# A kernel of sixteen sublayers: the set with logarithm and exponential loaded by an instruction, and the single layer norm in its wide form

## The reference

```python
def _layernorm(x, axis=-1, eps=1e-05):
    m = jnp.mean(x, axis=axis, keepdims=True)
    v = jnp.var(x, axis=axis, keepdims=True)
    return (x - m) / jnp.sqrt(v + eps)
```

```python
def _l2norm(x):                      # l0a, queries and keys
    return x * lax.rsqrt(jnp.sum(x * x, -1, keepdims=True) + 1e-06)
dt = jax.nn.softplus(jnp.einsum('blr,dr->bld', dt_r, W_dt) + b_dt)   # l0b
A = -jnp.exp(A_log)                                                  # l0b
o = (o - mean) * jax.lax.rsqrt(var + EPS)                            # l2a, per head
```

## Time and profile before

| | us |
|---|---|
| median of 3 runs | 3734.16 |
| lowest, highest | 3733.45, 3734.59 |
| profiled execution, its own time | 3737.65 |
| its span in the profile | 3735.9 |

### The profile page before, as it was taken

How to read it: one execution, slowest core, us unless ns; L and a number is a source line. 1 busy time by engine, 2 the same in 40 slices (tenths; PEclk the granted TensorE clock), 3 DMA queues, 4 the chain that set the end, 5 groups by cost and what they waited for, 6 DMA issues and landing times. The chain is left out here.

```text
span 3735.9 us, 56812 instructions
## 1 busy us (share of the span) xinstructions
PE 2940.7 (79%) x22174; PEld 1593.3 (43%) x22242; DVE 1930.9 (52%) x3686; ACT 1391.7 (37%) x2669; POOL 768.4 (21%) x629
## 2 busy tenths in 40 slices
PE   6566777778877599989768888998868568877986
PEld 4454247523356334444422223442333343664555
DVE  5311243478963488710588877113943543636643
ACT  3211533442233256632367776222032112224652
POOL 1000006245526200000554310004600000240003
PEclk9665869878889789999889999997989779878997
DMA  2022001122101422000121100002400001014202
GB/s 105 14 67 64 0 14 43 35 69 68 45 25 43 113 38 41 15 1 0 36 45 30 30 1 1 0 11 57 135 0 0 0 0 45 13 45 87 42 15 68
DMA packets 86478, 136.39 MB, mean 37 GB/s; under 512 B 13319, under 2 KB 52199, under 8 KB 84947
## 3 DMA queue, kind: packets, MB, share of 16 engines
q1 hardware_dynamic: 79187, 118.50, 12.6%
q0 software_dynamic: 7040, 14.43, 1.4%
HBM read 106.81 MB, written 25.85 MB: 36 GB/s over the span
## 5 line engine op out<-in xcount | busy, mean ns | idle before, releaser
L1674 DVE TENSOR_REDUCE at_mp<-PS 128x1 f32<-128x384 f32 (+3 forms) x640 | 313.4, 538 | 115.1 <-PE PS L1524 98.9
L1624 ACT ACTIVATE at_pt<-PS 128x384 f32<-128x384 f32 (+3 forms) x704 | 288.3, 456 | 211.9 <-PE PS L1536 176.7
L1521 PE MATMUL PS<-at_kx,at_qx 72*128 72x384 bf16 (+5 forms) x640 | 218.8, 347 | 67.1 <-DMA at_kx<-L_attn_a_parts 27.2
L1534 PE MATMUL PS<-at_qx,at_kx 105*128 105x512 bf16 (+5 forms) x704 | 214.3, 314 | 7.8 <-ACT at_pt L1624 5.9
L4159 DVE CUSTOM_DVE_ANT_0 PS<-PS,ls_pt 128x1024 f32<-128x1024 f32 x128 | 154.0, 1239 | 19.9 <-ACT ls_pt L4012 16.1
L4012 ACT ACTIVATE ls_pt<-PS,ls_far 128x512 f32<-128x512 f32 x256 | 155.6, 685 | 22.8 <-PE PS L3833 13.5
L2287 DVE TENSOR_TENSOR_SCAN mb_ring<-PS,mb_ring 128x1024 f32<-128x1024 f32 x64 | 146.6, 2291 | 19.3 <-POOL mb_ring L2226 6.6
L2242 PE MATMUL PS<-mb_ring,ident 128*128 128x512 f32 x256 | 148.1, 732 | 5.9 <-DVE mb_ring L2292 5.9
L1005 ACT ACTIVATE mx_h<-PS,small_L 128x128 f32<-128x128 f32 x312 | 87.9, 371 | 150.5 <-PE PS L889 63.8
L889 PE MATMUL PS<-mx_g,mx_w 128*128 128x128 f32 x624 | 98.4, 308 | 53.1 <-DVE mx_w L1082 30.6
L1547 PE MATMUL PS<-at_pt,at_v 128*9 128x256 f32 (+3 forms) x1408 | 130.8, 451 | 5.4 <-issue 1.3
(11 more groups left out here) (822 smaller groups left out, 6752.0 us busy)
## 6 DMA issues: line engine op xcount, KB each, us to landing
rw_arena<-rw_v_rows SPq DMA_DIRECT2D x32, 512.0 KB, 4.6
dl_arena<-in_fir_bank SPq DMA_DIRECT2D x32, 256.0 KB, 3.2
lnA<-mb_rows SPq DMA_DIRECT2D x16, 512.0 KB, 3.6
XN<-mb_rows SPq DMA_DIRECT2D x16, 512.0 KB, 3.7
ffn_place<-in_ffn_L SPq DMA_DIRECT2D x4, 1152.0 KB, 17.0
at_qx<-L_attn_a_parts SPq DMA_DIRECT2D x24, 192.0 KB
at_kx<-L_attn_a_parts SPq DMA_DIRECT2D x72, 64.0 KB
at_qx<-L_attn_b_parts SPq DMA_DIRECT2D x24, 192.0 KB
```

Source lines behind the costliest of these rows:

```text
L1521: mm = nc.tensor.matmul(PS[:, n % 3, 0:e - c], QX[0:RAW, u % 3, g, blk(i, P)], KX[0:RAW, u % 3, g, c:e], start=True, stop=True)
L1534: mm = nc.tensor.matmul(PS[:, 3 + n % 3, 0:e - c], KX[0:FULL, u % 3, g, blk(j, P)], QX[0:FULL, u % 3, g, c:e], start=True, stop=True)
L1624: nc.scalar.activation(PT[:, y % SLOTS, g, 0:e - c], PS[:, 3 + n % 3, 0:e - c], ACT.Exp, scale=SCALE).then_inc(exp_done, 1)
L1674: nc.vector.tensor_reduce(best, sc, AX.X, ALU.max).then_inc(s_maxed, 1)
```

## The change

The layer norm takes the form of the group norm: `center_mat` (the identity less 1/128) centres each block by one matmul, ACT squares out of PSUM, one matmul with `mean_mat` gives the variance on all partitions, ACT makes the logarithm and the exponential of 128x512, and DVE multiplies once.

```diff
@@ -95,6 +95,13 @@
         return scope.enter_context(self.nc.sbuf_tensor(f"{name}_{self.buffers}", shape, dt))
 
 
+LOG_AND_EXP = 6
+
+
+def load_log_and_exp(nc):
+    nc.scalar.add_instruction(mybir.InstLoadActFuncSet(act_func_set_id=LOG_AND_EXP, name=nc.get_next_instruction_name()))
+
+
 def turned_spread(nc, out, cols, ident):
 
     return nc.tensor.matmul(out, cols, ident, start=True, stop=True)
@@ -103,9 +110,8 @@
 def layernorm(k, src, dst, gain=None, shift=None, beside=None):
 
     nc, PS = k.nc, k.PS
-    sq, rstd = k.lnA, k.rstd
-    TB = BLK // P
-    with stage(nc, "mean_ready", "centered", "squared", "var_ready", "std_ready", "rstd_ready", "spread_ready", "scaled", "pool_own") as (block, mean_ready, centered, squared, var_ready, std_ready, rstd_ready, spread_ready, scaled, pool_own):
+    sq, rstd = k.lnA, k.lnA
+    with stage(nc, "centered", "squared", "var_ready", "log_done", "root_done", "scaled", "pool_own") as (block, centered, squared, var_ready, log_done, root_done, scaled, pool_own):
         if beside is not None:
             @block.gpsimd
             def _(pool):
@@ -113,42 +119,41 @@
 
         @block.tensor
         def _(pe):
+            def center(b):
+                nc.tensor.matmul(PS[:, b, :], k.center_mat[:, :], src[:, blk(b)], start=True, stop=True).then_inc(centered, 1)
+
             def variance(b):
                 pe.wait_ge(squared, b + 1)
-                for t in range(TB):
-                    mm = nc.tensor.matmul(PS[:, 4 + b, t:t + 1], sq[:, blk(TB * b + t, P)], k.mean_mat[:, 0:1], start=True, stop=True)
-                mm.then_inc(var_ready, 1)
-
-            def spread(b):
-                pe.wait_ge(rstd_ready, b + 1)
-                for t in range(TB):
-                    mm = turned_spread(nc, PS[:, b, blk(t, P)], rstd[:, TB * b + t:TB * b + t + 1].to_broadcast([P, P]), k.ident[:, :])
-                mm.then_inc(spread_ready, 1)
-
-            for b in range(NBLK):
-                nc.tensor.matmul(PS[:, b, :], k.mean_mat[:, :], src[:, blk(b)], start=True, stop=True).then_inc(mean_ready, 1)
+                nc.tensor.matmul(PS[:, 4 + b, :], k.mean_mat[:, :], sq[:, blk(b)], start=True, stop=True).then_inc(var_ready, 1)
+
+            center(0)
+            center(1)
             variance(0)
-            for b in range(1, NBLK):
-                variance(b)
-                spread(b - 1)
-            spread(NBLK - 1)
+            center(2)
+            variance(1)
+            center(3)
+            variance(2)
+            variance(3)
 
         @block.scalar
         def _(act):
             def square(b):
                 act.wait_ge(centered, b + 1)
-                nc.scalar.activation(sq[:, blk(b)], dst[:, blk(b)], ACT.Square).then_inc(squared, 1)
-
-            def deviation(b):
+                nc.scalar.activation(sq[:, blk(b)], PS[:, b, :], ACT.Square).then_inc(squared, 1)
+
+            def root(b):
                 act.wait_ge(var_ready, b + 1)
-                nc.scalar.activation(rstd[:, TB * b:TB * b + TB], PS[:, 4 + b, 0:TB], ACT.Sqrt, bias=k.eps_col[:, 0:1]).then_inc(std_ready, 1)
-
-            nc.scalar.activation(k.warm[:, 0:1], k.eps_col[:, 0:1], ACT.Sqrt)
+                nc.scalar.activation(rstd[:, blk(b)], PS[:, 4 + b, :], ACT.Ln, bias=k.eps_col[:, 0:1]).then_inc(log_done, 1)
+                act.wait_ge(log_done, b + 1)
+                nc.scalar.activation(rstd[:, blk(b)], rstd[:, blk(b)], ACT.Exp, scale=-0.5).then_inc(root_done, 1)
+
+            load_log_and_exp(nc)
             square(0)
-            for b in range(1, NBLK):
-                square(b)
-                deviation(b - 1)
-            deviation(NBLK - 1)
+            square(1)
+            for b in range(NBLK):
+                root(b)
+                if b + 2 < NBLK:
+                    square(b + 2)
             if gain is not None:
                 for b in range(NBLK):
                     act.wait_ge(scaled, b + 1)
@@ -156,30 +161,9 @@
 
         @block.vector
         def _(dve):
-            def center(b):
-                dve.wait_ge(mean_ready, b + 1)
-                nc.vector.tensor_tensor(dst[:, blk(b)], src[:, blk(b)], PS[:, b, :], ALU.subtract).then_inc(centered, 1)
-
-            def reciprocal(b):
-                dve.wait_ge(std_ready, b + 1)
-                nc.vector.reciprocal(rstd[:, TB * b:TB * b + TB], rstd[:, TB * b:TB * b + TB]).then_inc(rstd_ready, 1)
-
-            def scale(b):
-                dve.wait_ge(spread_ready, b + 1)
-                nc.vector.tensor_tensor(dst[:, blk(b)], dst[:, blk(b)], PS[:, b, :], ALU.mult).then_inc(scaled, 1)
-
-            center(0)
-            center(1)
-            center(2)
-            reciprocal(0)
-            center(3)
-            reciprocal(1)
-            scale(0)
-            reciprocal(2)
-            scale(1)
-            reciprocal(3)
-            scale(2)
-            scale(3)
+            for b in range(NBLK):
+                dve.wait_ge(root_done, b + 1)
+                nc.vector.tensor_tensor(dst[:, blk(b)], PS[:, b, :], rstd[:, blk(b)], ALU.mult).then_inc(scaled, 1)
 
 
 
@@ -2152,7 +2136,7 @@
                     take(b)
                     curve(b - 1)
                 curve(NBLK - 1)
-                nc.scalar.activation(k.warm[:, 0:1], k.eps_col[:, 0:1], ACT.Ln)
+                load_log_and_exp(nc)
                 nc.scalar.activation(A[:, :, :], W[pre + "A_log"], ACT.Exp).then_inc(own_a, 1)
                 keep(0)
                 for b in range(NBLK):
@@ -4282,9 +4269,8 @@
     def sb(n, shape, dt=F32):
         return k.sbuf(st, n, shape, dt)
     k.ident = sb("ident", [P, P])
-    k.mean_mat = sb("mean_mat", [P, P])
+    k.mean_mat, k.center_mat = sb("mean_mat", [P, P]), sb("center_mat", [P, P])
     k.eps_col = sb("eps_col", [P, 1])
-    k.rstd = sb("rstd", [P, NTILE])
     k.rstd2 = sb("rstd2", [P, 2, NTILE])
     k.tiny_col = sb("tiny_col", [P, 1])
     k.warm = sb("warm", [P, 1])
@@ -4312,6 +4298,8 @@
             own(pool.memset(k.ident[:, :], 0.0))
             own(pool.affine_select(out=k.ident[:, :], in_=k.ident[:, :], compare_op=ALU.not_equal, fill=1.0, base=0, pattern=[[-1, P]], channel_multiplier=1))
             own(pool.memset(k.mean_mat[:, :], 1.0 / D))
+            own(pool.memset(k.center_mat[:, :], -1.0 / D))
+            own(pool.affine_select(out=k.center_mat[:, :], in_=k.center_mat[:, :], compare_op=ALU.not_equal, fill=1.0 - 1.0 / D, base=0, pattern=[[-1, P]], channel_multiplier=1))
             own(pool.memset(k.eps_col[:, :], EPS))
             own(pool.memset(k.tiny_col[:, :], EPS * EPS))
             own(pool.iota(k.iota_row[:, :], [[1, 16]], base=0, channel_multiplier=0, allow_small_or_imprecise_dtypes=True))
```

## The result

The changed kernel took 3700.55 us in the median of six runs (3677.56 to 3705.31), the kernel before 3734.38 in six on the same chip: a ratio of 0.9901, with a 95% interval of 0.9880 to 0.9923: 33.8 us between the medians, 37 (29 to 45) by the ratio. The prediction was 3695.3, with 3680 to 3713. The profiled execution took 3704.39 us (span 3702.6) for 3737.65: 33.3 less, where the sum had said 38.9.

A forecast was written before the change was run, and what follows sets the result against it. No engine was near full; barrier-separated stages, each with its own last chain, bound the kernel. Terms summed to 38.9 us saved: profiled 3737.65 to 3698.8, or 3695.3 us at the median, range 3680 to 3713.

The forecast's parts named there:

- The norm: Fourteen layer norms: wide form ends at about +9.8 for +11.55 at the high clock; 22.0 us saved, bounds 12 and 26.
- a clock that falls inside the norms: Sign of being wrong: TensorE's granted clock dropping during the new norms; no size given.
- POOL's two stages: Norms of l1a and l1b: POOL's constants already end last, after the last scaling, so 0 us saved.
- The group norm: In l2a: seven table loads go, nearly all on ScalarE's chain; 7.3 us saved, bounds 5.5 and 8.5.
- The projection: In l0a: one load ahead of the wait replaces two per block; 5.6 us saved, bounds 3.8 and 7.
- The gates: In l0a: early load costs block 0 1.28 us, later blocks gain; 2.8 us saved, bounds 0 and 4.
- l0b: Warm-up logarithm and loads go, TensorE's chain starts 1.5 us earlier, VectorE becomes last; 5.2 us saved, bounds 3.5 and 7.
- l2b: Its loop keeps the set the norm leaves, so loads go; 2.6 us saved.
- The clock: Stages after norms: TensorE's 2.7 us rest lowers the clock; 8 stages x 0.75 us, 6 lost, bounds 0 and 14.
- The clock rivals: After norms: clock takes back 14 us, 3706 us, chance 0.20; or takes nothing back, 3685 us, chance 0.12.
- The slower one: Loads return before each logarithm and exponential of the norms: 120 us lost, 3854 us, chance 0.05.
- The drain: About 1.38 us extra per ScalarE table switch, making 2.66; would give 26 us more, about 3669; no chance given.

The follow-up runs named there:

- norm_two: Kernel before with the wide norm, its load and two unread matmuls behind the last variance, five other places unchanged: 3696.10 us, ratio 0.9894.
- loads_alone: Kernel before, narrow norm kept, with hand-placed table loads in the five other places: 3662.91 us, ratio 0.9899 to the kernel before.
- filler_two: Changed kernel plus two unread 128x512 matmuls behind each norm's last variance: 3636.97 us, ratio 0.9835 to the kernel before.
- after_again: Changed kernel itself, run again in a later sitting with a trace: 3661.51 us, ratio 0.9898 to the kernel before.
- before_again: Kernel before, unchanged, one run with a trace in a later sitting: 3706.34 us.

## Why the prediction was right, and where it was not

*The norm.* 20.0 for 22.0. The layout held to a tenth where the clock was high: five norms ended at +9.81 or +9.92 for +9.8. From the low clock seven ended at +11.99 to +12.76, where the text had +11.3 to +12.5. The other two, in front of l0b and l3a, started high and the clock fell inside them: from 702.50 to 704.50 us it was 0.50, behind that 0.99, and the norm ended at +11.4. The prediction had named a clock that falls inside the norms as a sign of being wrong. It did fall, in two of 14, at a cost of 1.5 us each; it had fallen inside two norms of the kernel before as well. Of the missing 2 us, 1.2 lie in one norm: the one at 2316 us starts low and ends at +12.76, where the one of before started high and ended at +11.55 (the earlier trace rows has its whole stretch up to the next stage, 12.00 us). POOL's two stages stayed at +17.1 and +15.6 as forecast.

*The group norm.* 9.2 for 7.3, above the bound of 8.5. The block cost was right (logarithms 1.73 apart). The step that was mis-sized is the delay of variance 3 behind the output matmul of block 0: I put the last logarithm at 2736.8, +11.0, and it is at +9.56, since that output matmul (2722.14) held variance 3 up by 0.4 us only: its square was done at 2722.73 and it starts at 2723.11.

*The projection.* 7.2 for 5.6, just above the upper bound of 7. Over all traces the stage took 66.4 to 68.8 us without the placed load (five) and 58.6 to 60.2 with it and without fillers (six), so the gain is rather 7 to 8: the second logarithm's wait that I had set against the loads took hardly anything from them (85.89 to 87.05 for both above), and the stage's mean clock was 0.81 for 0.78.

*The gates.* 0.1 for 2.8, the term that missed by most for its size. The early load takes 1.28 us in block 0, from 390.54 on, as I had it, but the copy behind it starts 35.9 us into the stage, for 33.9 before: 1.9 later. The gain of the later blocks did not make up for it: the stage lay at 146.0 to 146.8 in the kernel before and in four traces with the early load, at 140.9 to 141.2 in three others with it, and at 138.0 and 138.5 in both with the late load. (Of three other traces without a placed load here two have 146.1 and norm_two has 143.7.) Within the stage TensorE's clock falls and rises several times, at other places from trace to trace. That this parts 141 from 146 is what the clocks suggest; no run isolated it.

*l0b.* 4.6 for 5.2. With the same edits in it the stage took 53.0 to 53.1 us in six traces and 47.5 to 48.0 in three. The stretch from +28.5 to +37.5 of the stage in the changed kernel and in loads_alone (table by stage):

```profile
740.88:749.88 9.00, 9.00 (x11) 2.15 (x11) 2.30 (x4) 5.44 (x10) 0.00 (x0) 0.50 0.02 4
```

```profile
715.00:724.00 9.00, 9.00 (x18) 2.69 (x17) 4.90 (x9) 7.51 (x14) 0.00 (x0) 0.87 0.04 9
```

TensorE is busy throughout in both; at 0.50 it gets 11 matmuls done, at 0.87 18. In the three short traces the clock rises here, in the six others it stays at 0.50 up to +39. I had taken the matmuls of the earlier trace rows as low whatever happens ahead of them. That held in six of nine, and the bound of 7 was too low for the rest.

*l2b.* 3.6 for 2.6. The loop kept the set: the copy is now the stage's first entry (2851.64), where a load of 1.28 stood ahead of it. The first sequence gave 1.1 of its 1.28, since its eight matmuls took 6.47 us for 6.32, at the low clock in both kernels. The second gave 2.5, since its matmuls took 5.31 for 6.51: half of that gain is the clock's and was not forecast. At the high clock of filler_two the eight take 3.70.

*The clock.* The mechanism was right and its size was not: this is the term of the sum that was mis-sized. Against the kernel before, all else lost 10.7 us for 6, inside the bounds of 0 and 14. But the price of the rest itself is 24 us by the pairs with fillers. I had priced 8 stages at 0.75 us each; l2b's first alone paid 2.8, and the first l1_ffn took 166.3 in the changed kernel and 161.9 in filler_two (161.8 also in after_again, where its clock was up without fillers). And I had taken a drop in three of four rests, where 14 of 14 stages began low or half low in the first trace and 13 of 14 in each of its two repeats. How the 24 go with the 10.7 is told in part only. Some of them lie in the stages of other terms: l0b took 47.5 in filler_two and 53.0 in the changed kernel. That the kernel before had lost the rest in its own rests is not what the clock says: the mean of its first 3 us behind norms was 0.86 (0.82 in before_again), as in filler_two; no run fills the rests of the old norm. The norm alone came near its terms, 15.9 for 18.0, but on top of the loads only 5 were left, where the kernels with the narrow norm had the better clock inside gates and l0b, 10 us together. The sum treats its terms as independent, and the clock makes them depend on each other.

*The total.* That 3700.55 lies 5 us from 3695.3 is in part luck. The group norm, the projection and l2b gave 4.5 us more than forecast, and the norms, the gates, l0b and all else some 10 less.

*The rivals.* The clock rivals were about the right question with too small numbers. The slower one was the true price of the change without its one line: 115 for 120. The drain that the Trainium skill's page "ScalarE: Activation LUTs", section "What ACT_TABLE_LOAD costs", adds to each switch does not show in these traces: where ScalarE waits for nothing else, the next instruction starts within 0.02 us of the load's end, as at 2901.78 above.

## What to carry to other kernels

Where logarithm and exponential alternate, look for a table load between them in ScalarE's timeline, and place the set that has both once per stage: each load on a chain was 1.31 us, and in the 14 norms 112 of them were at stake. When a stage gets shorter by giving TensorE less to do, read the granted clock of the stage behind it; two unread matmuls that bridged 1.9 of 2.8 idle us were worth more than the rewritten norm. Don't add up what edits gave one by one: 15.9 and 37.4 us made 37 together. And place the load behind the last instruction that others wait for, not ahead of it.

## What the runs showed of the hardware

The rest that brought the low clock was short. In the norm shown, TensorE ended at +7.70 and rested for 3.8 us; the clock was still 0.99 in the 2.8 us behind that, and it was 0.50 from the next stage's first 3 us on; with 1.88 us of work in those 2.8 us it stayed at 1.00. Inside long stages the clock fell and rose at other places from trace to trace; l0b took 47.5 to 48.0 or 53.0 us with it.

The expert loop's two paces were not expected. Two rows of the waits from 565 to 680 us (us in total, times, longest us), of before and of before_again:

```profile
PEld PS L889 <- DVE mx_w L1082: 28.3, 15, 2.8
```

```profile
PEld PS L889 <- DVE mx_w L1082: 1.8, 5, 0.6
```

At the slow pace TensorE waits 15 times for VectorE's copy of the weights and the clock is 0.92; at the fast one it hardly waits and the clock is 1.00. Which is cause and which effect was not tried, nor what sets the pace. The spread of single runs is no mark of the change either: 28 us for the changed kernel in the first sitting, 5 for the kernel before; later 10 and 11 for the changed kernel and 13 to 32 for the kernel before.
